# Transposes of k and of the probabilities by DMA instead of TensorE, in a fused cross-attention and FFN kernel

## What is computed

```
x = x + attn(_layernorm(x), ctx);  x = x + ffn(_layernorm(x))
attn: q = rmsnorm((h @ Wq) per head, gq); k = rmsnorm((c @ Wk) per head, gk); v = (c @ Wv) per head
      scores = q k^T / sqrt(D); attn = softmax(scores); out = (attn @ v) @ Wo
ffn:  h = silu(bit_linear(x, w_gate)) * bit_linear(x, w_up); h = rms_norm(h, ln_weight); bit_linear(h, w_down)
bit_linear: activations rounded to 8 bits by row, weights rounded to -1, 0, 1 by their mean size
```

## Time and profile before

| | |
|---|---|
| median of 3 runs | 586.13 us (585.0 to 586.45) |
| profiled execution, its own time | 585.11 us |
| its span | 583.3 us |
| busy PE / PEld / DVE / ACT / POOL | 81% / 64% / 85% / 78% / 56% |
| HBM read, written | 14.16 MB, 2.10 MB |
| DMA, share of 16 engines (queue of SP) | 6.8% |

### The profile page before, as it was taken

The page is one execution under the profiler, slowest core; times in us unless marked ns, Lnnn a source line. Parts: engine busy times, 40 slices in busy tenths (PEclk is TensorE's granted clock), DMA queues, the critical chain, the costliest instruction groups (busy, mean ns, idle before and its releaser), DMA issues.

```text
span 583.3 us, 15141 instructions
## 1 busy us (share of the span) xinstructions
PE 470.0 (81%) x4968; PEld 372.8 (64%) x4968; DVE 494.0 (85%) x1125; ACT 455.1 (78%) x1495; POOL 328.3 (56%) x310
## 2 busy tenths in 40 slices
PE   0168375699999999999999999999998656668674
PEld 0156254588787877878788787878887532445453
DVE  3878889688988889888898888989889759999995
ACT  0269477599999999999999999999998545667573
POOL 1028335456766667677676677767777405545452
PEclk9989689799999999999999999999999995999899
DMA  7931401000000000000000000000000000000001
GB/s 292 333 96 51 166 1 34 4 1 1 0 0 0 0 0 0 0 0 0 0 0 0 0 0 0 0 0 2 2 3 1 1 2 1 9 26 21 18 29 46
DMA packets 10156, 16.60 MB, mean 28 GB/s; under 512 B 784, under 2 KB 7952, under 8 KB 9616
## 3 DMA queue, kind: packets, MB, share of 16 engines
q1 hardware_dynamic: 9024, 13.11, 6.8%
q10 hardware_dynamic: 1104, 3.15, 1.5%
HBM read 14.16 MB, written 2.10 MB: 28 GB/s over the span
## 4 chain that ended last, share of the span: by engine, by line
PE 40%; DVE 23%; issue 20%; POOL 9%; ACT 5%; DMA 1%; DVEq 1%; POOLq 0%; ACTq 0%
PE EB L340 10%; PE KQ L340 9%; PE SO L340 9%; PE TK L1050 3%; DVE pT L745 3%; POOL qshl L465 3%; POOL work L453 2%; DVE ham L866 2%; PE TM L1060 2%; DVE stage L936 2%; DVE kT L811 2%; DMA xs<-in_x 1%; PE TM L1026 1%; DVE wqs L877 1%; DVE qse L816 1%
## 5 line engine op out<-in xcount | busy, mean ns | idle before, releaser
L578 ACT ACTIVATE work<-SO,nbias,rq 128x128 f32<-128x128 f32 x256 | 114.3, 465 | 19.6 <-DVE nbias L784 15.3
L340 PE MATMUL KQ<-hT,wqs 128*128 (+1 forms) x1536 | 100.6, 224 | 15.9 <-DVE wqs L710 12.1
L459 POOL TENSOR_TENSOR rk<-kse,negh 128x4 f32<-128x4 f32 x64 | 65.3, 1021 | 85.1 <-DVE kse L776 85.1
L340 PEld LDWEIGHTS KQ<-hT,wqs 128*128 128x128 f16 x1536 | 94.5, 100 | 18.4 <-DVE wqs L710 7.7
L447 POOL TENSOR_TENSOR rq<-qse,negh 128x4 f32<-128x4 f32 x64 | 65.1, 1017 | 62.3 <-DVE qse L816 62.3
L340 PE MATMUL EB<-As,ohl 128*128 128x256 f16 x768 | 94.1, 272 | 0.0
L340 PEld LDWEIGHTS EB<-As,ohl 128*128 128x128 f16 x768 | 70.3, 97 | 8.6
L465 POOL TENSOR_TENSOR qshl<-work,qshl 128x512 f16<-128x512 f32 x64 | 74.1, 1158 | 0.0
L765 DVE SCALAR_TENSOR_TENSOR qhl<-KQ,gcol,qhl 128x512 f16<-128x512 f32 x64 | 48.0, 750 | 29.1 <-ACT qshl L551 28.1
L453 POOL TENSOR_TENSOR work<-work,rinv 128x512 f32<-128x512 f32 x64 | 66.5, 1039 | 6.8 <-DVE rinv L741 6.8
L558 ACT ACTIVATE kjunk<-KQ 128x128 f16<-128x128 f32 x256 | 68.0, 302 | 0.0
(11 more groups left out here) (158 smaller groups left out, 1049.5 us busy)
## 6 DMA issues: line engine op xcount, KB each, us to landing
xs<-in_x SPq DMA_DIRECT2D x4, 512.0 KB, 9.8
wvo<-in_wo SPq DMA_DIRECT2D x1, 2048.0 KB, 18.6
out<-wqs SPq DMA_DIRECT2D x16, 128.0 KB, 1.7
raw<-in_ctxT ACTq DMA_DIRECT2D x1, 1024.0 KB, 6.4
stage<-in_wk SPq DMA_DIRECT2D x1, 1024.0 KB, 12.5
stage<-in_wq SPq DMA_DIRECT2D x1, 1024.0 KB, 15.7
stage<-in_wq ACTq DMA_DIRECT2D x1, 1024.0 KB, 13.9
stage<-in_wgT SPq DMA_DIRECT2D x1, 1024.0 KB, 4.9
```

Source lines behind the costliest of these rows:

```text
L340: last = matmul(out, lhsT=left(i), rhs=right(j), start=start and n == 0, stop=stop and n == 2)
L459: pool.tensor_tensor(rk[:, s, :], kse[:, s, :], negh[:, 0:HG], ALU.pow).then_inc(rk_ok, 1)
L578: ins = act.activation(pe[:, s, c], SB[:, c], ACT.Exp, scale=rq[:, (g - AT_S) % 4, h:h + 1], bias=nbias[:, s, h:h + 1], accum_out=psm[:, s ...
```

## The change

PE's eight f32 transposes per step are gone. k is normalised as before into `kn` (DVE), then ACT rounds it to f16 (`khl`, high part), DVE makes the low part, and one DMA from SP transposes both parts, 128 partitions x 1024 f16, SBUF to SBUF, into `kT`. `pn` is now made by DVE, already scaled; DVE rounds it to f16 (`phl`), POOL makes the low part, and a second DMA transposes both into `pT`. SP runs through the steps in order: first the probabilities of group t-3, then the k of group t, each after a wait for its low part and for the matmuls that last read the buffer. On DVE and ACT the pair `ohl` moves from step t+5 to t+6, at the head of the step; on PE the probabilities x context go behind x A.

Around it: five weight splits stand ahead of step 0 instead of three, and steps 0 and 1 have two each; the remaining layernorms of x move to steps 4 to 9, the sums of the FFN's weights to steps 8 to 10; the loop begins at step 12 instead of 8 and still has twelve turns.

```diff
-AT_SSQ, AT_TK, AT_S, AT_TP, AT_O, AT_E = 1, 2, 3, 4, 5, 6
+AT_SSQ, AT_S, AT_O, AT_E = 1, 3, 5, 6
-LN_AT = {"start": (0, 2), 0: (2, 4), 3: (4, 6), 4: (6, 7), 5: (7, 8)}
+LN_AT = {"start": (0, 2), **{i + 2: (i, i + 1) for i in range(2, 8)}}
+LOOP_B = 3
-        SPLIT_AT = {"start": (0, 3), 0: (3, 5), 1: (5, 7), 2: (7, 9), 4: (9, 10), 5: (10, 11), 6: (11, 12)}
+        SPLIT_AT = {"start": (0, 5), 0: (5, 7), 1: (7, 9), 4: (9, 10), 5: (10, 11), 6: (11, 12)}
...
 SP:
+            for t in range(NT + 3):
...
+                if t >= 3:
+                    k = t - 3
+                    sp.wait_ge(plo_ok, k + 1)
+                    if k >= 2:
+                        sp.wait_ge(o_ps, k - 1)
+                    sp.dma_start_transpose(pT[:, k % 2, :, :].rearrange("p a (h n) -> p (a h) n", h=HG),
+                                           phl[:, k % 2, :, :].rearrange("p a n -> p (a n)")).then_inc(pT_in[k % 2], 16)
+                if t < NT:
+                    sp.wait_ge(klo_ok, t + 1)
+                    if t >= 2:
+                        sp.wait_ge(s_ps, t - 1)
+                    sp.dma_start_transpose(kT[:, t % 2, :, :].rearrange("p a (h n) -> p (a h) n", h=HG),
+                                           khl[:, t % 2, :, :].rearrange("p a n -> p (a n)")).then_inc(kT_in[t % 2], 16)
...
 POOL, step:
-                    need(pool, rinv_ok, b, g, 4)
-                    need(pool, pT_ps, b, g, 4, 2)
-                    pool.tensor_tensor(heads(pn[:, s, :]), heads(pe[:, s, :]), spread(rinv[:, s, :], SKV),
-                                       ALU.mult).then_inc(pn_ok, 1)
+                    need(pool, phi_ok, b, g, 4)
+                    need_dma(pool, pT_in[s], b, g, 4, 2)
+                    pool.tensor_tensor(phl[:, s, 1, :], pn[:, s, :], phl[:, s, 0, :],
+                                       ALU.subtract).then_inc(plo_ok, 1)
...
 ACT, step:
-                    act.activation(pT[:, s, 0, :], TPf, ACT.Copy, scale=P_SCALE).then_inc(phi_ok, 1)
+                if live(b, g, 1):
+                    s = (g - 1) % 2
+                    need(act, kn_ok, b, g, 1)
+                    need_dma(act, kT_in[s], b, g, 1, 2)
+                    act.copy(khl[:, s, 0, :], kn[:, s, :]).then_inc(khi_ok, 1)
...
 DVE, step:
-                    dve.scalar_tensor_tensor(out=pT[:, s, 1, :], in0=TPf, scalar=P_SCALE, in1=pT[:, s, 0, :],
-                                             op0=ALU.mult, op1=ALU.subtract).then_inc(pT_ok, 1)
+                    need(dve, rinv_ok, b, g, 4)
+                    need(dve, plo_ok, b, g, 4, 2)
+                    dve.scalar_tensor_tensor(out=heads(pn[:, s, :]), in0=heads(pe[:, s, :]), scalar=P_SCALE,
+                                             in1=spread(rinv[:, s, :], SKV), op0=ALU.mult,
+                                             op1=ALU.mult).then_inc(pn_ok, 1)
...
+                    need(dve, pn_ok, b, g, 4)
+                    need_dma(dve, pT_in[s], b, g, 4, 2)
+                    dve.tensor_copy(phl[:, s, 0, :], pn[:, s, :]).then_inc(phi_ok, 1)
...
-                    dve.tensor_copy(kT[:, s, 0, :], TKf).then_inc(khi_ok, 1)
+                if live(b, g, 1):
+                    s = (g - 1) % 2
+                    need(dve, khi_ok, b, g, 1)
+                    dve.tensor_tensor(khl[:, s, 1, :], kn[:, s, :], khl[:, s, 0, :], ALU.subtract).then_inc(klo_ok, 1)
...
-                    dve.tensor_tensor(kT[:, s, 1, :], TKf, kT[:, s, 0, :], ALU.subtract).then_inc(kT_ok, 1)
...
 PE, step:
-                        ins = te.transpose(TKf[:, c], kn[:, s, c], ident_f[:, :])
-                        ins = te.transpose(TPf[:, c], pn[:, s, c], ident_f[:, :])
```

More of the change, by code:

```diff
@@ L198, in build_program @@
         khi_ok = sem("khi_ok")
-        kT_ps = sem("kT_ps")
-        kT_ok = sem("kT_ok")
+        klo_ok = sem("klo_ok")
+        kT_in = [sem(f"kT_in{i}") for i in range(2)]
         q_ps = sem("q_ps")
@@ L215, in build_program @@
         phi_ok = sem("phi_ok")
-        pT_ps = sem("pT_ps")
-        pT_ok = sem("pT_ok")
+        plo_ok = sem("plo_ok")
+        pT_in = [sem(f"pT_in{i}") for i in range(2)]
         o_ps = sem("o_ps")
@@ L299, in steps @@
         def steps(eng, step, ffn):
-            straight(step, 0, 2 * G)
-            with eng.Fori(2, 2 + F_CHUNKS) as b:
+            straight(step, 0, LOOP_B * G)
+            with eng.Fori(LOOP_B, LOOP_B + F_CHUNKS) as b:
                 for g in range(G):
                     step(b, g)
-            straight(step, G * (2 + F_CHUNKS), FFN_AT)
+            straight(step, G * (LOOP_B + F_CHUNKS), FFN_AT)
             for s in range(G):
@@ L335, in need, with need_dma @@
                 eng.wait_ge(s, b * G + k)
+        def need_dma(eng, s, b, g, off, back=0):
+            k = g - off - back
+            if isinstance(b, int):
+                if G * b + k >= 0:
+                    eng.wait_ge(s, 16 * ((G * b + k) // 2 + 1))
+            else:
+                eng.wait_ge(s, b * (8 * G) + 16 * (k // 2 + 1))
         def pairs(matmul, out, left, right, start, stop):
@@ L466, in step @@
                                        ALU.subtract).then_inc(qslo_ok, 1)
[L467 to L470, removed]
+                if now(b, g) in C_AT:
+                    c_low(C_AT[now(b, g)])
+                if now(b, g) == 3:
+                    roots(1, B // XB)
                 if now(b, g) == PREP_AT:
@@ L536, in step @@
             def step(b, g):
-                ln_high(now(b, g) - 1 if now(b, g) > 0 else None)
[L538 to L541, removed]
-                    act.activation(pT[:, s, 0, :], TPf, ACT.Copy, scale=P_SCALE).then_inc(phi_ok, 1)
+                if live(b, g, AT_E):
+                    s = (g - AT_E) % 2
+                    need(act, o_ps, b, g, AT_E)
+                    need(act, e_ps, b, g, AT_E, 2)
+                    act.activation(ohl[:, s, 0, :], OB, ACT.Copy, scale=O_SHIFT).then_inc(ohi_ok, 1)
+                ln_high(now(b, g) - 1 if now(b, g) > 0 else None)
                 if live(b, g, 0):
@@ L582, in step @@
                 A_out(now(b, g))
-                if now(b, g) in range(B // XB):
-                    c_high(g)
+                if now(b, g) + 1 in C_AT:
+                    c_high(C_AT[now(b, g) + 1])
                 if now(b, g) in range(3, 7):
@@ L1021, in step @@
                         te.wait_ge(Ascl_ok, 1)
-                    if not isinstance(b, int) and g == 0:
+                    if now(b, g) == LOOP_B * G - 1:
                         te.wait_ge(wscl_ok, 1)
```

181 lines of the change are left out of this document (72 added, 109 removed).

## The result

The changed kernel takes 590.15 us (median of six runs, 587.52 to 592.76) against 586.08 of the kernel before in runs beside it (585.0 to 586.45): a ratio of 1.0069, 95% interval 1.0049 to 1.0089. Slower, as forecast, but by 4 us and not by 15; 601 was 11 too high, inside its range of 574 to 616. The profiled execution of after is the fastest of its six: span 585.7, its own time 587.52, against 583.3 and 585.11 before.

A forecast was written before the change was run, and what follows sets the result against it. The bound moves from PE to DVE: 4.87 us issue plus waits of 0.23, 0.77 and 0.20 is 6.07, taken as 6.15 against 5.95; +10.4 us over 52 steps and +5 startup give 601 us, range 574 to 616.

The forecast's parts named there:

- PE's relief: Steady step: PE loses 8 transposes, 0.88 us, but ACT at 5.6 us stops the step from shortening that much.
- the hold of low k on rk: Steady step: low k starts 0.05 us before POOL's rk and delays it; DVE waits 1.00 us before kn, mean 0.77.
- the startup: Before the steady steps: weight splits, sums and layernorms moved; between -3 and +10 us, taken as +5.
- a rinv that waits for the exponentials: DVE, steps whose ACT also rounds weights: a wait now and then, 0.1 us; step taken as 6.15 instead of 6.07.
- Rival B: Steady step: rk gets in before low k, ACT sets 5.70 us a step, 577 us in all; chance 0.24.
- whoever is first holds the other off: DVE and POOL: rule read from startup, where rk took 1.46 us instead of 1.01 after cTs started 0.16 before it.
- pn to its copy: DVE, steady step: the copy needs pn on the same engine; pn 0.60 us plus about 0.11 of wait behind it.
- the other blocking: Steady step: POOL's late qshl holds off pn or the next step's weight piece on DVE; 0.2 us per step.
- The base: Steady step of the kernel before: 5.95 us, from 42 runs of the line closing qhl in 250 us.
- The DMAs: Two transposing DMAs per step from SP: 2.2 to 4.9 us to landing, hidden, cost 0 unless the queue is too slow.
- C: Rival: the DMA queue is the bound, two transposes taking over 6.1 us; about 717 us at 4 us each; chance 0.08.
- D: Rival: PE, less busy, gets a clock of 0.73, so its work per step is 6.7 us; about 630 us; chance 0.04.

The follow-up runs named there:

- e1: The changed kernel with the small DVE operation qse moved ahead of low k; 569.50 us, 0.9718 of the kernel before.
- e4: The kernel before with one of four PE transposes left in each of the two groups, no DMA added; 573.50 us, ratio 0.9786.
- e2: The changed kernel with low k in its place but reading PSUM, so one SBUF operand instead of two; 574.05 us, 0.9791 of the kernel before.
- e3: The changed kernel with low k placed behind kn on DVE; 622.93 us, 1.0636 of the kernel before.
- e6: The changed kernel with the weight splits where the kernel before had them, three ahead of step 0; 593.01 us, 1.0110 of the kernel before.
- e0: The changed kernel run again unchanged, as control; 590.36 us, 1.0075 of the kernel before.
- e5: The changed kernel with a third transposing DMA of 256 KB in steps 8 to 63, into an unread buffer; 591.37 us, 1.0084 of the kernel before.

## Why the prediction was right in sign and wrong in size

The mechanism was right: PE's relief, ACT close behind it, and the hold of low k on rk. What failed are two terms of the sum. One is the startup, put at +5 us and measured at +0.3 in this pair. The other is the steady step, rounded up from 6.07 to 6.15 for a rinv that waits for the exponentials, a wait that did not occur; the step is 6.03. The net was small, a gain of about 13 us against a loss of about 17, so that errors of a few microseconds set the number.

**PE's relief, and the bound that comes next: right.** Rival B's step, ACT at 5.70, is near what e1 shows, 5.72. e4, which takes PE's work alone, lands at 5.72 as well.

**rk is held by low k: right, and it decides the sign.** Forecast: low k starts 0.05 before rk, kn 1.85 after kse, rk mean 1.35, three steps in four. Measured: 0.01 to 0.10, 1.78 to 1.87, 1.37, 31 of 42. What the startup's two neighbouring cases of cTs and rk had shown held to a tenth of a microsecond, and e1 and e2 show that this is the cause. Here the Trainium skill ("SBUF — State Buffer", section "SBUF: two separate sides") lets whichever operation starts first have the shared port for its whole instruction and blocks the other. The runs agree where the first one is long: 1.51 against 1.01 for rk with two SBUF operands in low k (after), 1.01 with one (e2), and 1.03 against 0.68 for low k behind POOL's qshl (e3). They disagree where the first one is rk: in e1 low k starts 0.10 into rk and takes its usual 0.69, so rk doesn't keep it off for its whole time. The sentence "whoever is first holds the other off" in the prediction is too wide in the same way, and the earlier trace rows had the case. The recorded starts don't decide to the last hundredth either: in step 14 of after low k starts 0.01 us behind rk, and rk takes 1.56. In e1, where low k starts 0.09 us or more behind rk, rk is free in every one of these steps.

**The sign had little to spare.** In one of three held steps low k led by 0.01 to 0.02 us. Had rk been free there, 0.5 us in one of four steps would be about 6 us in fifty (an estimate from these figures), and the change would have been slightly faster than the kernel before. Forecasting one lead of 0.05 for all of them was right in the outcome and partly lucky.

**The steady step: wrong by 0.12 of 6.15.** The sum itself was 6.07, and the fifty steps gave 6.03. Then I rounded it up to 6.15 for a rinv that waits for the exponentials; no wait of DVE for ACT is in the list of that stretch; ACT, 46.52 of 50 busy, is done in time. In e1, where the step is 5.72, this wait exists, 3.8 us in 44 steps. The top-up is the largest part of the step's error: 0.08 x 52 = 4.2 us. Within the sum terms were off and nearly cancelled: pn to its copy took 0.72 to 0.83 instead of 0.72, and xs waited 0.26 for PE in one step of four, which the sum has not; the other blocking, put at 0.2, shows in the timeline of these fifty steps mainly as a weight piece of 0.50 instead of 0.33 in one step of four, 0.04 per step.

**The base: 5.95 was low by 0.02.** 42 executions in 250 us are a count with two cut ends; from the 14th to the last start it is 298.70 / 50 = 5.97. That is 1.2 us of the 10.4. A difference of 0.2 per step can't rest on a base read to a whole count.

**Startup: +5 forecast, +0.3 in this pair of profiles.** x lands 1.15 us later in the profile of after, so the change itself takes 0.8 us off. The forecast had two parts. The first, 3.5 us lost ahead of the first q and given back by step 3, failed: nothing is lost, and the splits' new order is worth 2.5 us (e6 against after, e0 and e5). The second, sums and layernorms that cost more in steps 8 to 10 than they save earlier, was right in sign: with the old splits (e6) the startup is 7.2 us ahead of before at step 7, 2.4 behind at step 11, and 1.7 behind at step 13. So this part, together with what the new steps themselves do in the startup, costs 1.7 and not 5. And before's steps there took 9.3, 7.1 and 5.7 us, not "near 6" (from one start of qhl to the next, steps 7 to 10).

**Together:** +15.4 forecast, +2.4 in the profiled pair. The 13.0 between them are 6.4 from the new step, 1.2 from the base, 4.7 from the startup, 0.6 from the tail, 0.1 from 52 steps where I now count 50. The median moved by 4.1, since the profiled run of after is its fastest.

**The DMAs: right.** Landing took 3.1 to 3.3 us and not 2.2, inside the bounds of 2.2 to 4.9, and it is hidden with another 50% on top (e5). C, the queue as the bound, is out. So is the table of the Trainium skill ("VectorE: DVE Perf Modes", section "The three transpose paths"), if taken as a price per block: 1309 ns for each of eight blocks would be 10.5 us, and the trace has 3.1 to 3.3 for all eight.

**The clock: right.** With PE 42.28 of 50 us busy it was 1.00, all at 2.4 GHz, so D didn't occur. Between 475 and 500 it was 0.83 (in five windows of 5 us: 0.79, 0.87, 1.00, 1.00, 0.50), a mean of stretches at 2.4 and 1.2 GHz. That is higher than in the same window of before, 0.73, though PE was less busy, and the tail was no longer.

**B had 0.24.** It gave e1's step (5.70 against 5.72), for a kernel one 0.2-us operation away from this one, but not its time, 577 against 569.5, mainly as it carried the same +5 of startup (e1's fifty steps took 12.8 us less than before's). For this kernel the order of starts was read rightly.

## What to carry to other kernels

Where VectorE and GpSimd run side by side, take the timeline of before and put every VectorE operation with two SBUF operands next to the GpSimd operation that starts near it. Here the one that started first decided whether a 1.0-us operation took 1.5, and if someone on the critical path waits for it, half a microsecond per step is won or lost by moving a small, harmless operation in between. When a change moves work from a full engine to others and the time hardly moves, look for one new wait, not for many small costs, and price the relief by itself on the kernel before. Count steps between two starts, not in a window, and take off the landing of the first load before two startups are compared.

## What was not expected

- Leads of 0.01 to 0.10 us were worth 21 us of 590 (e1 against e0), and came out alike in the same 38 of the last 51 steps in four profiles: this race is stable, not noise.
- The changed kernel spreads more than the one before: 587.5 to 592.8 in six runs, 588.8 to 592.0 in e0, against 585.0 to 586.45 (the kernel before had one run of 588.76 later). Its steady steps repeat within 0.2 us. The startup differs almost only by the landing of x; the tail, 136.5 to 141.4 us over after, e0 and e5, has no cause that I know.
- One transposing DMA of 256 KB, SBUF to SBUF in f16, holds SP's queue for 1.24 us and lands after 3.1 to 3.3. The 128 of them raised the packets from 10,156 to 145,325, nearly all under 512 B, and kept the 16 engines 44% busy in the steady stretch.
- e3: placing low k behind kn, seemingly out of everyone's way, cost 32.6 us over e0, as DVE then both waited for POOL (1.06 us) and was held by it (1.03 instead of 0.68).
